# A cross-attention and feed-forward kernel on one core: the first values' load is split from the first keys' load, and three low parts of the input are formed one to two groups later

## What is computed

```python
x = x + xattn(layernorm(x), ctx, mask, position_bias, ln_weight, w_q, w_k, w_v, w_out)
x = x + ffn(layernorm(x), weight, bias, gate_w, in_channel_scale, out_channel_scale)

def xattn(hidden, kv, ...):
    q = (rmsnorm(hidden, ln_weight) @ w_q.T).reshape(b, lq, H, DH)
    k = (kv @ w_k.T).reshape(b, lk, H, DH)
    v = (kv @ w_v.T).reshape(b, lk, H, DH)
    score = softmax(where(mask, einsum("bqhd,bkhd->bhqk", q, k) + position_bias, -inf))
    return hidden + einsum("bhqk,bkhd->bqhd", where(mask, score, 0), v) @ w_out.T
```

## Time and profile before

| | us |
|---|---|
| median of 3 runs | 852.41 (852.15 to 853.0) |
| profiled execution | 852.58 |
| its span in the profile | 850.8 |
| TensorE busy in it | 837.7 (98%) |
| VectorE busy | 622.6 (73%) |
| ScalarE busy | 390.9 (46%) |
| GpSimd busy | 302.8 (36%) |

### The profile page before, as it was taken

How to read it: one execution, slowest core, us unless ns; L and a number is a source line. 1 busy time by engine, 2 the same in 40 slices (tenths; PEclk the granted TensorE clock), 3 DMA queues, 4 the chain that set the end, 5 groups by cost and what they waited for, 6 DMA issues and landing times.

```text
span 850.8 us, 12849 instructions
## 1 busy us (share of the span) xinstructions
PE 837.7 (98%) x4356; PEld 703.6 (83%) x4356; DVE 622.6 (73%) x1003; ACT 390.9 (46%) x1007; POOL 302.8 (36%) x279
## 2 busy tenths in 40 slices
PE   9999999999999999999999999999999999999997
PEld 8878888888888877888888888888888888888875
DVE  5787846778775786877777777877777787787665
ACT  5632422432431444544554554455455445446762
POOL 2013211022030143625445543544554354444225
PEclk9999999999999999999999999999999999999997
DMA  8445464573353759414224313422431342150002
GB/s 253 155 164 196 156 227 136 180 260 127 133 174 112 222 172 313 141 56 152 79 80 152 111 62 142 152 85 75 152 119 65 132 151 97 63 210 8 1 25 75
DMA packets 60720, 114.07 MB, mean 134 GB/s; under 512 B 5208, under 2 KB 38872, under 8 KB 55408
## 3 DMA queue, kind: packets, MB, share of 16 engines
q1 hardware_dynamic: 60656, 113.25, 38.9%
HBM read 77.58 MB, written 35.65 MB: 133 GB/s over the span
## 4 chain that ended last, share of the span: by engine, by line
PE 83%; DVE 7%; issue 4%; POOL 2%; ACT 2%; DMA 1%; POOLq 0%; DVEq 0%; ACTq 0%; SPq 0%
PE out L1296 10%; PE out L1298 10%; PE out L1297 10%; PE proj L1296 8%; PE proj L1298 8%; PE proj L1297 8%; PE o L1387 6%; PE s L1368 6%; PE s L1298 3%; PE s L1297 3%; PE s L1296 3%; PE t L1376 3%; PE s L1344 1%; POOL acc L790 1%; DMA w_stage<-in_wq 1%
## 5 line engine op out<-in xcount | busy, mean ns | idle before, releaser
L889 ACT ACTIVATE probs<-probs,neg_max 128x128 f32<-128x128 f32 x256 | 99.7, 391 | 133.2 <-DVE neg_max L1143 133.1
L728 POOL TENSOR_TENSOR w_stage<-w_stage 128x256 f32<-128x256 f32 x30 | 26.6, 886 | 311.8 <-DMA w_stage<-in_wk 150.4
L740 POOL TENSOR_TENSOR w_lo<-w_stage,w_hi 128x512 fp32r<-128x512 f32 (+1 forms) x52 | 59.7, 1159 | 140.3 <-ACT w_hi L827 140.3
L1296 PE MATMUL out<-wo_hi,o_hi 128*128 128x512 f32 x224 | 95.1, 425 | 0.6 <-DVE acc L1177 0.6
L1177 DVE TENSOR_TENSOR acc<-out,acc 128x512 f32<-128x512 f32 x100 | 68.6, 688 | 36.2 <-PE out L1298 36.1
L1296 PE MATMUL proj<-x_hi,w_hi 128*128 128x512 f32 x210 | 88.6, 422 | 0.2 <-DVE ring L1002 0.2
L1298 PE MATMUL out<-wo_lo,o_hi 128*128 128x512 f32 x224 | 88.3, 394 | 0.0
L1297 PE MATMUL out<-wo_hi,o_lo 128*128 128x512 f32 x224 | 87.6, 391 | 0.0
L1298 PE MATMUL proj<-x_lo,w_hi 128*128 128x512 f32 x210 | 82.7, 394 | 0.0
L1297 PE MATMUL proj<-x_hi,w_lo 128*128 128x512 f32 x210 | 82.0, 391 | 0.0
L752 POOL TENSOR_TENSOR bias_mask<-bias_raw,mask_neg 128x512 f32<-128x512 f32 x64 | 77.0, 1215 | 11.0 <-DVE probs L1140 10.9
(11 more groups left out here) (352 smaller groups left out, 2151.1 us busy)
## 6 DMA issues: line engine op xcount, KB each, us to landing
k_spill<-ring SPq DMA_DIRECT2D x64, 256.0 KB, 2.8
v_spill<-ring SPq DMA_DIRECT2D x64, 256.0 KB, 2.2
w_stage<-in_wk SPq DMA_DIRECT2D x32, 256.0 KB, 3.3
big_stage<-in_wv SPq DMA_DIRECT2D x8, 1024.0 KB, 7.6
w_stage<-in_wq SPq DMA_DIRECT2D x32, 256.0 KB, 4.3
k_first<-k_spill SPq DMA_DIRECT2D x8, 1024.0 KB, 6.7
v_first<-v_spill SPq DMA_DIRECT2D x8, 1024.0 KB, 4.8
wo_raw<-in_wo SPq DMA_DIRECT2D x16, 512.0 KB, 3.3
```

The lines of the kernel that those rows point to most:

```text
L740: pool.tensor_tensor(lo, staged(m, part), hi.bitcast(F32), ALU.subtract).then_inc(g_wlo, 1)
L889: last = act.activation(probs[:, j % 2, b, :], probs[:, j % 2, b, :], ACT.Exp, bias=neg_max[:, col:col + 1], accum_out=row_sum[:, col:col ...
L1296: pe.matmul(to[:], left_hi, right_hi, start=first and n == 0, stop=False, skip_group_check=True)
```

## The change

Two things. The steps XX 3, 5 and 4 go from (29, 4), (29, 6), (30, 1) to (30, 3), (31, 0), (31, 2). The step "KV" is split into "KL" (keys) and "VV" (values). Biases and keys of head pair 0 go from (31, 1) to (31, 4), its values to (32, 1), behind the DMAs of weights 17. For all later pairs "VV" follows "KL" at once, as before; only the waits for saved values are now asked for between them.

```diff
     put(k + 5, 1, ("XX", 6))
     put(k + 5, 3, ("XT", "T4"))
-    put(k + 5, 4, ("XX", 3))
-    put(k + 5, 6, ("XX", 5))
-    put(k + 6, 1, ("XX", 4))
-
-    put(k + 7, 1, ("BL", 0), ("BL", 1), ("KV", 0))
+    put(k + 6, 3, ("XX", 3))
+    put(k + 7, 0, ("XX", 5))
+    put(k + 7, 2, ("XX", 4))
+
+    put(k + 7, 4, ("BL", 0), ("BL", 1), ("KL", 0))
+    put(k + 8, 1, ("VV", 0))
...
-            def keys_and_values(p):
+            def attention_keys(p):
                 if p >= NPAIR:
                     return
                 saved(group_at["K", p])
-                for t in range(HALF):
-                    saved(group_at["V", p // 4, t])
...
                 sp.dma_start(k_tiles[p % 2][:], k_spill[p]).then_inc(d_k[p % 2], 16)
+
+            def attention_values(p):
+                if p >= NPAIR:
+                    return
+                for t in range(HALF):
+                    saved(group_at["V", p // 4, t])
                 if p >= 2:
                     sp.wait_ge(pe_pv, last_score(p - 2))
                 sp.dma_start(v_tiles[p % 2][:], v_spill[p]).then_inc(d_v[p % 2], 16)
```

More of the change, by code:

```diff
@@ L180, in schedule @@
     put(q + 1, 0, ("S", 0), ("EXP", 0))
-    put(q + 1, 1, ("KV", 1))
+    put(q + 1, 1, ("KL", 1), ("VV", 1))
     put(q + 1, 3, ("N", 0), ("BL", 2), ("WO", 0))
@@ L256, in schedule @@
             steps += [("S", 4), *prod[7], *prod[3], ("T", 3), ("EXP", 4), ("BM", 5), ("BL", 4), *prod[4],
-                      *outs(0, 0), ("N", 4), ("KV", 2), *sums, ("PV", 3), *outs(0, 1, 2)]
+                      *outs(0, 0), ("N", 4), ("KL", 2), ("VV", 2), *sums, ("PV", 3), *outs(0, 1, 2)]
             continue
@@ L263, in schedule @@
         split_output = [("WO", p + 1)] if 2 * p + 2 == SPLIT else []
-        steps += slot(j + 3, prod[4] + outs(p, 0), outs(p, 1), outs(p, 2), [("KV", p + 2), *sums, *split_output])
+        steps += slot(j + 3, prod[4] + outs(p, 0), outs(p, 1), outs(p, 2), [("KL", p + 2), ("VV", p + 2), *sums, *split_output])
     j = 2 * SPLIT
@@ L707, in store @@
                 sp.dma_start(out[i], acc[:, i, :]).then_inc(d_out, 16)
-            walk({"WL": pair_weights, "DL": second_plain_pair, "VL": value_weights, "SAVE": save, "ML": mask_load, "XL": x_load, "KV": keys_and_values,
+            walk({"WL": pair_weights, "DL": second_plain_pair, "VL": value_weights, "SAVE": save, "ML": mask_load, "XL": x_load, "KL": attention_keys, "VV": attention_values,
                   "BL": bias_load, "WOL": output_weights, "AL": residual_load, "SMALL": small_loads, "FW": ffn_weights, "SUM": store})
```

## The result

| | before | after |
|---|---|---|
| median of 21 runs each | 853.92 us | 855.91 us |
| span of the profiled execution | 850.8 us | 853.9 us |
| product 1 of K14 to S1 | 39.04 us | 40.59 us |

The ratio is 1.0026, with a 95% interval of 1.0016 to 1.0036: the change makes the kernel 0.26% slower, where 852.4 (850.4 to 853.5) was forecast. The first three runs of the kernel before had a median of 852.41; over 21 runs it is 853.92.

What follows compares the result with a forecast made beforehand. TensorE, busy 98%, was taken as the bound, so only its waits count. The -0.74 us at 303 us is eaten by a new wait and longer later ones: 0.0 at S1, so 852.4 against the median 852.41, range 850.4 to 853.5.

Steps and rivals of the forecast that it cites:

- the ceiling: Three TensorE waits around 300 to 345 us, with their slower restarts, hold 2.7 us, the most the change could win.
- Part 1: Moving the three XX out of cycles 29 and 30 lets the awaited `w_lo` come earlier: -0.74 us near 303 us.
- gap B: TensorE's wait for `w_lo` at 302.86 to 303.75 us, 0.66 us too long, behind an `x_lo` on VectorE.
- Part 2: The moved XX lengthen VectorE's queue in cycle 31: the read L1006 starts at 318.6 instead of 315.75.
- gap F: A new TensorE wait for `w_lo` of weights 16 near 319.5 us, put at 0.3 us (0 to 0.6).
- stretch of 0.87: VectorE's moved XX 4 and `tail_lo` meet GpSimd's sums of weights 16 and take 0.33 + 0.54 us longer.
- slower rival: Three VectorE instructions in cycle 31 each wait out a whole GpSimd sum; weights 17 land at 331.1, time 854.5; 7%.
- Part 3: On SyncE the keys wait behind saves and go out at 321.2 (320.4 to 321.5), over 5 us later than 315.85.
- Part 4: In the DMA queue, with values behind weights 17, row 0 lands at 329.0 (327.5 to 330.0), before 328.98.
- The sum: Scores S1 at 329.0 + 4.7 + 5.6 = 339.3, a change of 0.0 us, ends -1.5 and +1.0.
- two faster rivals: Weights 17 land by 326.8, all waits go, 850.2 (20%); or near 327.5 to 328.3, half the gain, 851.3 (25%).
- signs named for "wrong": `k_first` issued by SyncE before 320, or weights 17 landing before 327.5, would show the forecast wrong.

Runs made afterwards that it cites:

- e2: Changed kernel with the three XX, biases and keys back at their old places, only the first values behind weights 17; 850.87 us beside 853.07 for the kernel before.
- e7: Changed kernel with biases and keys back at (31, 1) and XX 3, 5, 4 at (29, 6), (30, 3), (30, 6); 851.17 us beside 853.38 before.
- e9: Changed kernel with the first keys moved to (32, 1), behind weights 17, and the first values to (32, 5); ratio to the kernel before 1.0021.
- e11: Changed kernel with biases and keys back at (31, 1) and XX 3, 5, 4 at (29, 6), (30, 1), (30, 3); 852.03 us beside 854.17 before.
- e5: Changed kernel with only XX 5 moved, from (31, 0) to (30, 6); ratio to the kernel before 0.9999.
- e12: The changed kernel run again unaltered, for a second execution with a trace; ratio to the kernel before 1.0017.
- e8: Changed kernel with only the first values moved on, from (32, 1) to (32, 5); ratio to the kernel before 1.0039.
- e10: Changed kernel with biases and keys moved from (31, 4) to (31, 2), in front of two saves; ratio to the kernel before 1.0022.
- e1: Changed kernel with the first values back in front of weights 17, at (31, 4) right behind the keys; ratio to the kernel before 1.0058.
- e3: Changed kernel with only the two bias loads moved, from (31, 4) to (32, 1), behind weights 17; ratio to the kernel before 1.0011.

## Why the prediction was wrong, point by point

**What bounds the kernel, and the ceiling**: right up to S1. e2 and e7 reached S1 at -1.55 and -2.3 against 39.04, within the 2.7 us of the gaps. That a microsecond won there is kept to the end holds only roughly: e9 has S1 0.4 earlier and is 0.21% slower, and e11 has S1 1.9 earlier and is faster by 0.13%, which its interval does not tell from nothing.

**Part 1, gap B**: right. It went, -0.74.

**Part 2, VectorE in cycle 31**: right to 0.1 us. XX 5 was to begin at 313.08 and began at 313.20, L1006 (now L1011) at 318.6 and 318.68, gap F at 0.3 and 0.25. But the rule of the Trainium skill (SBUF — State Buffer, section "SBUF: two separate sides") was set aside wrongly. XX 4 at 317.00 met a sum that GpSimd had begun at 316.61:

```profile
316.61 1.06 POOL L735 TENSOR_TENSOR w_stage<-w_stage 128x256 f32<-128x256 f32 x1
317.64 1.72 POOL L736 TENSOR_TENSOR w_stage<-w_stage 128x256 f32<-128x256 f32 x1
```

XX 4 was stretched by 0.54, and ended 1.08 behind the end of that sum (317.67), about what it takes by itself; the next sum, begun in the midst of XX 4, took 1.72 instead of 0.74, and ended 0.6 behind XX 4. By that rule, one engine holds the shared ports for a whole instruction and the other waits; these rows and the `w_lo` of e7 agree. The 128x4 row of e7 is not explained by it, for the sum that it ended with began behind it. The stretch of 0.87 in the forecast came out (0.26 for `tail_lo`, 0.54 for XX 4) though the rule holds, since what VectorE paid in these two meetings was the rest of the sum in progress and not a whole sum, as the slower rival had it.

**Part 3, keys on SyncE**: right. Forecast 321.2, measured 321.27; row 0 issued at 322.6 and 322.90. e5 shows the path from VectorE's queue to the keys, one for one.

**Part 4, the landing of weights 17: the step that failed.** The term "`k_first` takes 5.1 us", with ends of 4.8 and 5.8 ("I take 5.1, nearer the short end, since nothing large follows it"), measured 6.6 and 7.3. The term behind it, one save and two rows at 2.7, measured 2.8 and, in e12, 2.1. Together, from the issue of the keys to the landing of row 0, 9.4 us in both executions in place of 7.8, with a far end of 8.5. So 321.3 + 6.6 + 2.8 = 330.7 in place of 329.0, outside the end of 330.0. The fault of the estimate is plain. The earlier trace rows give 4.8, 6.7 and 7.6 for the eight loads of `k_first`; I took the smallest as one end and left the median out, for I held "nothing large behind it" to be a gain. No row said that, and the runs deny it: e8, with still less behind the keys, has 6.8, and e2, e7 and e11 have 6.5 to 6.6. Why the load takes 6.6 here and 5.8 in the kernel before is open. A second term was charged at nothing, the transfers issued ahead of the keys after a dry stretch. The queue rate of 0.9 us for 256 KB came from a queue that was running; the changed kernel lets it run dry (nothing moved from 317 to 320) and then starts it anew, 2.30 us to the first landing. But that this start is what lengthens the keys' load is not shown: in e2 the keys take 6.5 with no such pause ahead of them, and in e10 6.8 with two of the saves no longer ahead of them. (The Trainium skill, DMA: Bandwidth & Descriptors, section "Anatomy of one DMA — SWDGE (gpsimd) path", gives each DMA a fixed part of about 2 us besides its bytes; the 2.30 for a save of 256 KB into an empty queue is not far from it, though these DMAs are issued by SyncE.)

**The sum.** S1 was to stand at 339.3, 0.0 against before, and stood 1.55 later (rel; 1.1 by the second execution of before). From the landing of row 0 to S1 it was 10.31 us, as forecast (4.7 + 5.6), so the miss at S1 is the landing's alone. The medians differ by 2.0. Where the rest, some 0.5 us, arises is not shown; the stage of attention varies by more than that by itself: from S1 to the last scores it is 449.98 and 452.32 us in the two executions of before, 451.69 and 451.13 in those of after. The last scores in the second execution of before, and in after:

```profile
791.75 1.06 PE L1368 MATMUL s<-k_second,ring 128*128 128x128 f32 x8
```

```profile
792.70 1.06 PE L1373 MATMUL s<-k_second,ring 128*128 128x128 f32 x8
```

A further 1.5 us of the miss is the base: 852.41 in three runs, 853.92 in 21. So 852.4 + 1.5 + 2.0 = 855.9.

**The rivals.** The slower rival (7%) named the decision point and the size right (row 0 later than 329.0 costs, beyond the band from 330.7; 854.5 against 852.41, +2.1). Its place and its cause were others: not VectorE and L1011, which came as forecast, but the queue behind it. The two faster rivals (45%) needed row 0 at 328.3 or less and are what e2 and e7 do, where the keys go out at rel 15, not 21. The chance of "slower" was too small, since the largest unknown, the keys' load, had its ends on one side. Both signs named for "wrong" looked to that side too (keys out before 320, row 0 before 327.5).

## What to carry to other kernels

A queue in order passes a delay on to all that stands behind: ask of every step moved into "idle" time on one engine which DMA waits for the read behind it, and what that DMA keeps back. Time in which the transfer queue is dry is lost to it, and here the smaller load in front did not bring it back (1.0 MB put off, 1.4 MB behind). Price a block of transfers from its first issue, and by the median of its own rows, not by the shortest. Split a change that has two parts, for here one half gained 0.2% and the other lost more.

## What the runs showed of the hardware that was not expected

- **Clock.** TensorE's granted clock fell to half after an idle time of 5.13 us (e1) and also after 2.40 us in e8, while it stayed at 1.00 after 2.29 (after), 2.24 (e12), 2.68 (e10) and 2.71 us (e3). The idle time of the row alone does not tell which of the two comes. In e8 the matmuls then started every 0.43 us for 3.9 us, and S1 came 0.7 us later than in the changed kernel. TensorE in e8 (with busy time by stretches, clock third from the end), and in e10:

```profile
332.00:335.50 3.50, 3.50 (x13) 2.95 (x13) 2.03 (x3) 1.48 (x3) 3.50 (x5) 0.54 0.70 197
...
331.73 0.73 PE L1301 MATMUL out<-x_hi,w_hi 128*128 128x512 f32 x1 [2.40 <-DVE w_lo L1023]
332.26 0.63 PE L1302 MATMUL out<-x_hi,w_lo 128*128 128x512 f32 x1
332.69 0.63 PE L1303 MATMUL out<-x_lo,w_hi 128*128 128x512 f32 x1
```

```profile
331.77 0.47 PE L1301 MATMUL out<-x_hi,w_hi 128*128 128x512 f32 x1 [2.68 <-DVE w_lo L1023]
332.07 0.40 PE L1302 MATMUL out<-x_hi,w_lo 128*128 128x512 f32 x1
```

- **VectorE behind GpSimd.** An operation of 128x4, 0.17 us by itself, took 1.58, and a `w_lo` of 0.68 took 2.29 (e7). Both ended with an instruction of GpSimd (345.34 + 1.15 = 346.49, 339.59 + 2.86 = 342.45 and 0.54 more for the `w_lo`'s own work), so the price goes by GpSimd's instruction and not by VectorE's own. I take this to be why the stage of attention differs by 2.3 us between two executions of one kernel; that was not tested by itself.
